# Attention's end reordered, attn_out into bank 2, and VectorE's background pieces ahead of the third mask

## The chip, the cores and the metric

The kernel runs on one core of one Trainium2 chip. The metric is the device time of one execution in microseconds (us); lower is better. TensorE (PE) multiplies and transposes into eight PSUM banks, VectorE (DVE), ScalarE (ACT) and GpSimd (POOL) do the elementwise work, and SyncE (SP) issues the DMAs. Each engine takes its instructions strictly in program order and waits on counting semaphores.

## The reference

One decoder layer on x of shape (4, 512, 512): causal attention with 32 query heads in 8 key groups, a cross product with a quantised context, and a mixture of experts. Cut to what matters:

```
x = x + attn(layernorm(x)):   q, k, v = x @ wq, x @ wk, x @ wv; rope on q and k
                              out = softmax(mask(q k^T / 8)) v, heads joined, @ wo
x = x + xattn(layernorm(x)):  8-bit rounding of x in blocks of 128 and of the context
                              in blocks of 128x128, then the product of the two
x = x + moe(layernorm(x)):    probs = softmax(xt @ Wg); eidx = argmax; place in its expert's
                              256 rows; silu(xd W1) * (xd W3) @ W2, plus the same of a
                              shared expert (sw1, sw3, sw2)
```

## The kernel before

**Attention** is a loop over `h` in `range(NH + 7)`, NH = 128, written out once for each engine; I call one value of `h` a step. A head is one batch and one four-head group's query head; four heads make a unit (`NU` = 32). Head `h` goes down a pipeline that is spread over several steps. On TensorE a step holds, in this order: `scores(h, 3)` and `scores(h, 2)` (banks 0 and 1), two thirds of the step's projection for a later unit, `weigh(h - 3)` (probabilities times values, bank 5), `turn_p(h - 2, 0)` (the probabilities of head h-2 turned, first of three parts, into bank 2), `scores(h, 1)`, `turn_p(h - 2, 1)` (bank 3), `scores(h, 0)`, `turn_p(h - 2, 2)` (bank 4), the rest of the projection, and `attn_out(h - 7)`, which multiplies a finished tile by wo. The steps whose unit index ends a cycle (k = 0, where k = (h + 8) mod 4) also turn the values (`turn_v`, L512). Steps with h of 120 and more have no projection. An fp32r product is made of three matmuls (`three`, L484 to L486).

**The banks of `attn_out`.** It writes bank 5, the bank of `weigh`, and bank 7 from n = NH - 11 = 117 on. So before it writes, `join` of head h-3 must have read bank 5 (`wait_bank5`), and before the next `weigh` writes, VectorE's `attn_out` (the add to X, L1269) must have read it.

**VectorE's step** is: `inverse_sums(h - 1)`, then the background pieces of some steps (`context_max`, `steps_of`, `large_steps_of`, `look`, the scales), then `masked(h, 3)`, `masked(h, 2)` (L1219, which ScalarE's `exp` waits for), per-unit work (`key_cos`, `value_lo`, `rotate`, `split_wo_lo`), `masked(h, 1)`, `join(h - 3)` (L1254, reads bank 5 and what ScalarE's `lower_out` left in Otmp), a side slot, `pt_lo(h - 2, 0)` (L1260, the last reader of bank 2), `masked(h, 0)`, `pt_lo` of parts 1 and 2, `rotate`, and the add of `attn_out(h - 7)`.

**The side slots** hold the later stages, batch by batch: `slots()` is a table of slot numbers for each stage. From step 117 on each step runs two slots (numbers 2(h - 117) - 44 and - 43), the first of them between `join` and `pt_lo(h - 2, 0)`. After the loop come slots -8, -7, -6, and then one slot with each eighth of a half batch `x` of the shared expert. `stats2` are row statistics for the second layernorm, `norm2` its root, `look` and `peaks` its block maxima, `scales`, `scaled` and `cross_round` the rounding (GpSimd does the last three operations, L1703 to L1707), `cross_turn` and `cross_product` the product with the context. Context jobs and the rounding for batch 0 run as a background during steps 59 to 124.

The weights of the shared expert are split into a high and a low part in pieces (`split_piece`), two in each step after h = 130 and the rest after the loop.

Of the kernel before, what the change touches and what calls it, by code (L numbers as in the profile page):

```python
# [10 lines left out]
NU = NG * NB  # L11
# [24 lines left out]
def slots():  # L36
# [17 lines left out]
    plan(-2, "logits", 0)  # L54
    plan(0, "choose", 0)
    plan(3, "place", 0)
    for b in range(1, NB):
        s = 16 * (b - 1)
        for i in range(TB):
            plan(s - 13 + i, "stats2", b, i)  # L60
            if b > 1:
                plan(s - 4 + i + i // 3, "context_turn", b, i)
# [16 lines left out]
        plan(s + (19 if b < NB - 1 else 15), "place", b)  # L79
    for i in range(2):  # L80
        plan(16 * NB - 13 + i, "load_x", i)
        plan(16 * NB - 9 + i, "expert_turn", 0, i)
# [20 lines left out]
def decoder(nc, x_in, ctx_in, wqkv_in, wo_in, wg_in, wf_in, ident_in, mask_in, rope_in, ksin_in, rank_in, tri_in, out):  # L103
# [3 lines left out]
    with ExitStack() as root:  # L107
# [170 lines left out]

        def set_of(x):
            return 0 if x < NX else x - NX + 1  # L280
# [38 lines left out]
        PT_BLOCKS = [[(0, qb) for qb in range(4)], [(1, 1), (1, 2), (1, 3), (3, 3)], [(2, 2), (2, 3)]]  # L319

# [61 lines left out]
        def wait_piece_free(need, m, p):  # L382
            if m == 0 and p < UP:
                need.wait_ge(p_pv, NH)
            elif m == 0:
                wait_attention(need)
# [34 lines left out]
        def wait_bank5(need, h, user):  # L421

            if user == "attn_out":
                need.wait_ge(a_tmp, h - 2)
                need.wait_ge(v_join, h - 2)
            elif h < 8 or h - 8 >= NH - 11:
                need.wait_ge(a_tmp, h - 3)
                need.wait_ge(v_join, h - 3)
            else:
                need.wait_ge(v_x, h - 7)  # L430
# [39 lines left out]
        def tensor_engine(e):  # L470
# [68 lines left out]
            def weigh(h):  # L539
# [7 lines left out]
                wait_bank5(need, h + 3, "weigh")  # L547
# [21 lines left out]
            def attn_out(n):  # L569
# [3 lines left out]
                ps = bank[7 if late else 5][:, :]  # L573
# [3 lines left out]
                if not late:  # L577
                    wait_bank5(need, n + 7, "attn_out")
                elif n == NH - 11:
                    wait_part(need, NU - 1, 2)  # L580
                else:
                    need.wait_ge(v_x, n)
# [101 lines left out]
            def ffn(x, k):  # L684
# [8 lines left out]
                if k < 6:  # L693
# [3 lines left out]
                    if x == 0 and k < 3:  # L697
                        wait_attention(need)
# [41 lines left out]
            for h in range(NH + 7):  # L740
# [32 lines left out]
                if 52 <= h < 60:  # L773
                    need.wait_ge(a_pt, 3 * (h - 2) + 1)
                    need.wait_ge(v_pt, 3 * (h - 2) + 1)
                    first_turn(h - 44, 2)
# [14 lines left out]
        def scalar_engine(e):  # L791
# [117 lines left out]
            def look_later(b, i):  # L909

                need.wait_ge(v_small, 3 + 2 * b)
                if i == 3:
                    need.wait_ge(p_kv, NU)
                    need.wait_ge(g_t2, TB * (b - 1))
# [70 lines left out]
            def split_piece(m, p):  # L985
                n = NP * m + p
                need.wait_ge(d_ring[n % NR], 16 * (n // NR + 1))
                wait_piece_free(need, m, p)
# [11 lines left out]
            def ffn(x, k, split):  # L1000
                m = set_of(x)
                if k < 6:
# [4 lines left out]
                    if x == 0 and k < 2:  # L1007
                        wait_attention(need)
# [37 lines left out]
            for h in range(NH + 7):  # L1046
# [53 lines left out]
                if 52 <= h < 60:  # L1100
                    first_turn(h - 44, 2)
                if h >= SIDE:
                    side_slot(2 * (h - SIDE) - 43)
                if h > NH + 2:
                    for _ in range(2):
                        split_piece(0, pieces.pop(0))
            for s in (-8, -7, -6):
                side_slot(s)
            while len(pieces) > NP - UP:
                split_piece(0, pieces.pop(0))  # L1110
            need.wait_ge(d_k, 48)
            need.wait_ge(g_const, 1)
            e.activation(Gh[:, :, 0:8], Graw[:, :, :], ACT.Copy).then_inc(a_const, 1)
            e.activation(trib[:, :], tri[:, :], ACT.Copy, accum_out=code[:, TB:TB + 1]).then_inc(a_const, 1)
# [14 lines left out]
        def vector_engine(e):  # L1129
# [133 lines left out]
            def attn_out(n):  # L1263
# [5 lines left out]
                e.tensor_tensor(X[:, t, :], X[:, t, :], bank[7 if n >= NH - 11 else 5][:, :], ALU.add).then_inc(v_x, 1)  # L1269
# [152 lines left out]
            def side_slot(s):  # L1422
                ends = []
                for x in side.get(s, ()):
# [7 lines left out]
                    elif stage in ("norm2", "rstd3"):  # L1432
                        rstd_of(slice(b * TB, (b + 1) * TB))
                        if stage == "norm2":
                            bias_of(b)
                    elif stage == "peaks":
# [112 lines left out]
            for h in range(NH + 7):  # L1549
# [4 lines left out]
                if h >= 0 and h % 8 == 0 and 0 < h // 8 + 1 <= NSAVE:  # L1554
                    split_wq_lo(h // 8 + 1)
                if h in takes:
# [11 lines left out]
                if 0 <= h < NH:  # L1568
                    masked(h, 3)
                    masked(h, 2)  # L1570
                if after_unit and k == 0:
# [602 lines left out]
```

## Time and profile before

| | us |
|---|---|
| three runs | 1531.92, 1531.93, 1536.74; median 1531.93 |
| the profiled execution | 1532.62, of which its instructions span 1530.8 |
| PE busy | 1437.9 (94%) |
| DVE, ACT, POOL busy | 1147.5 (75%), 984.9 (64%), 1027.0 (67%) |

Times in the rows are microseconds from the start of the profiled span. "Busy" of PE is modelled and its matmuls overlap, so the start-to-start distance of two matmuls says more than their duration. The arrow in square brackets names what ended an engine's idle time. One step of attention is the distance between two starts of the first `scores` matmul (L502, 128x512).

### The profile page before, as it was taken

What the parts mean: (1) busy time and instruction counts of PE and PEld (TensorE: products, weight loads), DVE (VectorE), ACT (ScalarE), POOL (GpSimd) and SP (SyncE); (2) the same over time, 40 slices, a digit from 0 to 9 for tenths busy, and PEclk for the clock granted to TensorE, in tenths of its full rate; (3) what the DMA queues carried; (4) which work ended last, traced back from release to release, by engine and by line L of the source; (5) the groups of instructions that cost most, each with busy time, mean ns of one, the idle gap of its engine ahead of it and who ended that gap; (6) DMA issues with size and microseconds to landing.
All of it is one profiled execution on the core that took longest, in us unless ns stands there. A gap on an engine that the chain in (4) does not pass through costs nothing.

```text
span 1530.8 us, 26938 instructions
## 1 busy us (share of the span) xinstructions
PE 1437.9 (94%) x8617; PEld 1259.0 (82%) x8617; DVE 1147.5 (75%) x2820; ACT 984.9 (64%) x2509; POOL 1027.0 (67%) x1043
## 2 busy tenths in 40 slices
PE   5899999999999999999999999897898999999997
PEld 3778888888878888778888888776787888999996
DVE  7678888887887887887888788787565754677773
ACT  4687786777776887878878787756141412555562
POOL 3787888888877788888898888644404131366663
PEclk9999999999999999999999999999999999999998
DMA  6445454334322424334234342504111011587772
GB/s 209 116 122 166 124 147 134 87 111 124 84 80 63 112 75 128 88 83 123 73 113 126 82 132 66 169 1 147 43 35 49 22 43 39 170 267 236 253 244 80
DMA packets 108620, 174.74 MB, mean 114 GB/s; under 512 B 20936, under 2 KB 42696, under 8 KB 108480
## 3 DMA queue, kind: packets, MB, share of 16 engines
q1 hardware_dynamic: 104448, 160.51, 36.0%
q0 software_dynamic: 3840, 12.25, 2.1%
q8 instruction: 70, 1.15, 0.3%
q14 instruction: 70, 0.57, 0.1%
q10 hardware_dynamic: 192, 0.26, 0.1%
HBM read 94.05 MB, written 33.18 MB: 83 GB/s over the span
## 4 chain that ended last, share of the span: by engine, by line
PE 66%; ACT 12%; DVE 11%; issue 5%; DMA 2%; POOL 2%; SPq 1%; DVEq 0%; POOLq 0%; ACTq 0%
PE bank L484 15%; PE bank L486 14%; PE bank L485 14%; PE bank L536 5%; ACT P L875 5%; PE bank L551 4%; PE bank L552 3%; PE bank L502 3%; PE bank L503 3%; DVE P L1219 2%; ACT PTh L887 2%; PE bank L476 2%; ACT Otmp L881 2%; DVE PTl L1260 1%; DVE Opair L1254 1%
## 5 line engine op out<-in xcount | busy, mean ns | idle before, releaser
L875 ACT ACTIVATE P<-P,mn 128x512 f32<-128x512 f32 (+3 forms) x512 | 284.5, 557 | 206.9 <-DVE mn L1219 203.1
L1660 POOL TENSOR_TENSOR P<-P,ri 128x128 f32<-128x128 f32 (+3 forms) x512 | 360.7, 737 | 30.7 <-DVE ri L1208 30.7
L1219 DVE CUSTOM_DVE_ANT_0 P<-bank,mask 128x512 f32<-128x512 f32 (+3 forms) x512 | 236.6, 480 | 84.3 <-PE bank L503 82.8
L1260 DVE TENSOR_TENSOR PTl<-bank,PTh 128x512 fp32r<-128x512 f32 (+1 forms) x384 | 229.8, 599 | 34.1 <-ACT PTh L887 31.1
L536 PE MATMUL bank<-ident,P 128*128 128x128 f32 x1280 | 202.6, 273 | 2.5 <-POOL P L1660 2.5
L887 ACT ACTIVATE PTh<-bank 128x512 fp32r<-128x512 f32 (+1 forms) x384 | 198.1, 517 | 3.9 <-PE bank L536 1.0
L502 PE MATMUL bank<-KT,QT 128*128 128x256 f32 (+2 forms) x512 | 188.1, 368 | 6.4 <-DVE mn L1219 6.4
L484 PE MATMUL bank<-XT,Wh 128*128 128x512 f32 x384 | 163.8, 427 | 8.1 <-DVE XT L1190 3.5
L503 PE MATMUL bank<-KT,QT 128*128 128x256 f32 (+2 forms) x512 | 166.0, 324 | 0.0
L551 PE MATMUL bank<-PTh,VS 128*128 128x256 f32 (+2 forms) x512 | 161.1, 326 | 5.2 <-DVE X L1269 2.4
L552 PE MATMUL bank<-PTl,VS 128*128 128x256 f32 (+2 forms) x512 | 154.5, 324 | 0.0
L486 PE MATMUL bank<-XT,Wl 128*128 128x512 f32 x384 | 152.9, 398 | 0.0
L485 PE MATMUL bank<-XT,Wh 128*128 128x512 f32 x384 | 152.6, 397 | 0.0
L536 PEld LDWEIGHTS bank<-ident,P 128*128 128x128 f32 x1280 | 150.1, 141 | 3.0 <-POOL P L1660 3.0
L1698 POOL TENSOR_TENSOR OTl<-Opair,OTh 128x512 fp32r<-128x512 f32 x64 | 83.6, 1306 | 94.7 <-ACT OTh L958 93.9
L484 PE MATMUL bank<-Oh,OTh 128*128 128x512 f32 x256 | 106.0, 414 | 20.9 <-DVE Opair L1254 15.5
L1254 DVE TENSOR_TENSOR Opair<-bank,Otmp 64x512 f32<-64x512 f32 x128 | 87.4, 683 | 39.8 <-ACT Otmp L881 38.5
L502 PEld LDWEIGHTS bank<-KT,QT 128*128 128x128 f32 x512 | 96.8, 189 | 21.2 <-DVE mn L1219 8.9
L1011 ACT ACTIVATE hm<-bank 128x256 f32<-128x256 f32 x96 | 36.4, 379 | 117.8 <-PE bank L486 117.0
L551 PEld LDWEIGHTS bank<-PTh,VS 128*128 128x128 f32 x512 | 96.2, 188 | 19.4 <-issue 6.7
L503 PEld LDWEIGHTS bank<-KT,QT 128*128 128x128 f32 x512 | 97.5, 190 | 10.5
L552 PEld LDWEIGHTS bank<-PTl,VS 128*128 128x128 f32 x512 | 96.1, 188 | 10.0
(225 smaller groups left out, 4090.2 us busy)
## 6 DMA issues: line engine op xcount, KB each, us to landing
RW<-in_wf SPq DMA_DIRECT2D x153, 256.0 KB, 3.4
QT<-qh SPq DMA_DIRECT2D x256, 64.0 KB, 2.0
QT<-ql SPq DMA_DIRECT2D x252, 64.0 KB, 2.0
Oraw<-in_wo SPq DMA_DIRECT2D x16, 512.0 KB, 4.8
KT<-KT SPq DMA_DIRECT2D x32, 256.0 KB, 3.0
Wraw<-in_wqkv SPq DMA_DIRECT2D x9, 768.0 KB, 4.7
xnx<-in_ctx SPq DMA_DIRECT2D x24, 256.0 KB, 3.5
saved<-Wh SPq DMA_DIRECT2D x7, 768.0 KB, 3.5
```

The costliest lines, as they stand in the source:

```text
L484: e.matmul(ps, lh, rh, start=start, stop=False)
L485: e.matmul(ps, lh, rl, start=False, stop=False)
L486: return e.matmul(ps, ll, rh, start=False, stop=stop)
L502: e.matmul(ps[:, 0:k], lhs, KT[:, u % 2, 0, 0:k], start=True, stop=False)
L503: e.matmul(ps[:, 0:k], lhs, KT[:, u % 2, 1, 0:k], start=False, stop=True).then_inc(p_s, 1)
L536: last = e.transpose(ps[:, tokens(m)], src, ident[:, :])
L551: e.matmul(ps[:, q:512], lhs, pt_of(PTh, kb), start=kb == 0, stop=False)
L552: last = e.matmul(ps[:, q:512], lhs, pt_of(PTl, kb), start=False, stop=kb == 3)
L875: e.activation(pq, pq, ACT.Exp, bias=mn[:, z, qb:qb + 1], scale=-1.0, accum_out=rs[:, z, qb:qb + 1]).then_inc(a_exp, 1)
L1219: e.tensor_tensor_reduce(P[:, z, off[qb]:off[qb] + k], bank[n % 2][:, 0:k], mask[:, 512 - k:512], -0.125, BIG, ALU.add, ALU.min, mn[:, z, ...
L1260: e.tensor_tensor(pt_part(PTl, part), bank[2 + part][:, 0:128 * n].rearrange("p (m n) -> p m n", n=128), pt_part(PTh, part).bitcast(F32), ...
L1660: e.tensor_tensor(pq, pq, ri[:, z, qb:qb + 1].to_broadcast([128, n]), ALU.mult).then_inc(g_norm, 1)
```

## The change

- **Output bank.** `attn_out` writes bank 2 (`out_bank`) for n < 117, then bank 7, and for n = 125 and 127 bank 2 again. Before it writes bank 2 it waits for both readers of `turn_p(n + 5, 0)`: in step h that is `pt_hi` and `pt_lo` of head h-2, part 0. The next step's `turn_p(.., 0)` waits for VectorE's add, and `weigh` for `join` of the head before it alone.
- **VectorE's step.** The masks 3 and 2 come first. The add (now of tile h - 8, for n < 117), the per-unit work, and then the background pieces stand between mask 2 and mask 1.
- **First turns** of steps 52 to 59 go to bank 5 in place of bank 2.
- **Batch 1's side stages** are planned apart: `stats2` in slots -44, -42, -40, -38 (steps 117 to 120) in place of -13 to -10; the root is started on VectorE in slot -36 and finished by GpSimd's `newton` in slots -34 to -28; `look` at -14, `peaks` at -12, `scales` at -8 in place of -8, -7 and -4; the four roundings one or two slots sooner. `logits`, `choose` and `place` of batch 0 move from -2, 0, 3 to -6, -4, -2.
- **Pieces and constants.** Eleven pieces are split in steps 128 to 133. The router's weights and constants are loaded in step 125 and prepared in steps 128 to 130, and a first Silu is run in step 129.

The core of the diff (the slot table, `pieces_at`, `bias_of` on GpSimd and the waits on counts that go with them are left out):

```
+        def out_bank(n):
+            return bank[2 if n < NH - 11 or n >= NH - 4 and n % 2 else 7]
...
@@ turn_p
-                if part == 0 and 51 <= h < 59:
-                    wait_xt(need, h - 42)
+                if part == 0 and 0 <= h - 6 < NH - 11:
+                    need.wait_ge(v_x, h - 5)
@@ weigh
-                wait_bank5(need, h + 3, "weigh")
+                wait_bank5(need, h + 3)
@@ attn_out on TensorE
-                ps = bank[7 if late else 5][:, :]
+                ps = out_bank(n)[:, :]
...
                 if not late:
-                    wait_bank5(need, n + 7, "attn_out")
+                    need.wait_ge(a_pt, 3 * (n + 5) + 1)
+                    need.wait_ge(v_pt, 3 * (n + 5) + 1)
                 elif n == NH - 11:
                     wait_part(need, NU - 1, 2)
-                else:
+                elif n <= NH - 4:
                     need.wait_ge(v_x, n)
+                else:
+                    need.wait_ge(a_pt, 3 * NH)
+                    need.wait_ge(v_pt, 3 * NH)
+                    need.wait_ge(v_x, n - 1)
@@ ScalarE's loop
+                if h == NH + 1:
+                    need.wait_ge(d_k, 48)
+                    need.wait_ge(g_const, 1)
+                    e.activation(Gh[:, :, 0:8], Graw[:, :, :], ACT.Copy).then_inc(a_const, 1)
+                    e.activation(trib[:, :], tri[:, :], ACT.Copy, accum_out=code[:, TB:TB + 1]).then_inc(a_const, 1)
+                    e.activation(wam[:, 0, 0:1], wam[:, 0, 0:1], ACT.Silu)
@@ VectorE's loop
+                if 0 <= h < NH:
+                    masked(h, 3)
+                    masked(h, 2)
+                if 0 <= h - 8 < NH - 11:
+                    attn_out(h - 8)
+                if after_unit and k == 0:
+                    key_cos(unit - 1)
...
                 if h in takes:
                     context_max(takes[h])
...
-                if 0 <= h < NH:
-                    masked(h, 3)
-                    masked(h, 2)
...
-                if 0 <= h - 7 < NH:
+                if NH - 11 <= h - 7 < NH:
                     attn_out(h - 7)
```

How the order stands now. First VectorE in step 106, before and then after the change (`ISA` is the mask, L1219 before and L1259 after; PTl<-bank2 is `pt_lo` part 0; X<-X,bank5 or bank2 is the add):

```order
L1208 RECIPROCAL ri<-rs 128x4 [waits a_exp]
L1219 ISA P,mn<-bank0,mask 128x512 [waits p_pt,p_s]
L1219 ISA mn 128x1
L1219 ISA P,mn<-bank1,mask 128x384 [waits p_s]
L1219 ISA mn 128x1
L1232 TENSOR_TENSOR qcs<-bank6,rope 128x512
L1219 ISA P,mn<-bank0,mask 128x256 [waits p_s]
L1219 ISA mn 128x1
L1254 TENSOR_TENSOR Opair<-bank5,Otmp 64x512 [waits a_tmp]
L1260 TENSOR_TENSOR PTl<-bank2,PTh 128x512 [waits p_pv,a_pt]
```

```order
L1248 RECIPROCAL ri<-rs 128x4 [waits a_exp]
L1259 ISA P,mn<-bank0,mask 128x512 [waits p_pt,p_s]
L1259 ISA mn 128x1
L1259 ISA P,mn<-bank1,mask 128x384 [waits p_s]
L1259 ISA mn 128x1
L1309 TENSOR_TENSOR X<-X,bank2 128x512 [waits v_x,p_ao]
L1272 TENSOR_TENSOR qcs<-bank6,rope 128x512
L1259 ISA P,mn<-bank0,mask 128x256 [waits p_s]
L1259 ISA mn 128x1
L1294 TENSOR_TENSOR Opair<-bank5,Otmp 64x512 [waits a_tmp]
L1300 TENSOR_TENSOR PTl<-bank2,PTh 128x512 [waits p_pv,a_pt]
```

The add, which stood ahead of the reciprocal, stands behind mask 2; `join` and `pt_lo` keep their place behind mask 1.

TensorE at the end of a step, before and after (bank 4 and 6 are the last turned part and the projection, Oh with OTh is `attn_out`):

```order
L536 MATMUL bank4<-ident,P 128x128 x2
L484 MATMUL bank6<-XT0,Wh 128x512
L485 MATMUL bank6<-XT0,Wh 128x512
L486 MATMUL bank6<-XT0,Wl 128x512
L484 MATMUL bank5<-Oh,OTh 128x512 [waits v_join,a_tmp]
L485 MATMUL bank5<-Ol,OTh 128x512
```

```order
L563 MATMUL bank4<-ident,P 128x128 x2
L511 MATMUL bank6<-XT0,Wh 128x512
L512 MATMUL bank6<-XT0,Wh 128x512
L513 MATMUL bank6<-XT0,Wl 128x512
L511 MATMUL bank2<-Oh,OTh 128x512 [waits v_pt,a_pt]
L512 MATMUL bank2<-Ol,OTh 128x512
```

The output keeps its place in TensorE's order; its wait moved from `join` to the `pt_lo` that stands behind `join` on VectorE.

VectorE in step 118 after the change (before it, the two middle rows stood near the loop's end):

```order
L1294 TENSOR_TENSOR Opair<-bank5,Otmp 64x512 [waits a_tmp]
L1202 BN_STATS st<-X 128x6
L1204 BN_AGGR mv<-st 128x2 [waits v_own]
L1300 TENSOR_TENSOR PTl<-bank2,PTh 128x512 [waits p_pv,a_pt]
L1259 ISA P,mn<-bank1,mask 128x128 [waits p_s]
```

Batch 1's statistics now stand between `join` and the `pt_lo` that `attn_out` waits for.

## Rows read from the trace of the kernel before

**Rows 1.** Windows: stretch, its length, busy PE, PEld, DVE, ACT, POOL, PEclk, DMA, GB/s.
```profile
98.90:951.60 852.70, 832.46 (x4739) 715.35 (x4738) 696.98 (x1843) 662.79 (x1751) 720.41 (x761) 1.00 0.38 106
...
1012.50:1049.00 36.50, 27.86 (x151) 22.78 (x150) 31.17 (x70) 18.96 (x40) 16.00 (x16) 0.95 0.20 61
1049.00:1098.70 49.70, 40.06 (x233) 35.26 (x234) 32.93 (x78) 21.09 (x50) 23.20 (x27) 0.93 0.26 80
```

**Rows 2.** Waits in 98.9 to 951.6, TensorE's, then VectorE's: total, times, longest.
```profile
PE bank L484 <- DVE Opair L1254: 13.7, 26, 1.2
PE bank L484 <- DVE XT L1190: 2.0, 1, 2.0
DVE P L1219 <- PE bank L503: 67.7, 80, 2.0
```

**Rows 3.** Timeline, TensorE: first turn in step 57; first matmuls of steps 104 to 108.
```profile
474.24 0.60 PE L476 MATMUL bank<-ident,xnx 128*128 128x128 f32 x4
...
831.68 0.39 PE L502 MATMUL bank<-KT,QT 128*128 128x512 f32 x1
...
839.40 0.39 PE L502 MATMUL bank<-KT,QT 128*128 128x512 f32 x1
...
846.51 0.39 PE L502 MATMUL bank<-KT,QT 128*128 128x512 f32 x1
...
853.64 0.39 PE L502 MATMUL bank<-KT,QT 128*128 128x512 f32 x1
...
861.19 0.39 PE L502 MATMUL bank<-KT,QT 128*128 128x512 f32 x1
```

**Rows 4.** Timeline, step 105: mask 1, join, pt_lo part 0, and TensorE's attn_out.
```profile
843.75 0.42 DVE L1219 CUSTOM_DVE_ANT_0 P<-bank,mask 128x256 f32<-128x256 f32 x1 [1.19 <-PE bank L503]
...
844.10 0.68 DVE L1254 TENSOR_TENSOR Opair<-bank,Otmp 64x512 f32<-64x512 f32 x1
...
844.70 0.67 DVE L1260 TENSOR_TENSOR PTl<-bank,PTh 128x512 fp32r<-128x512 f32 x1
...
845.13 0.39 PE L484 MATMUL bank<-Oh,OTh 128*128 128x512 f32 x1
```

**Rows 5.** Timeline, step 106: join, pt_lo part 0, and attn_out.
```profile
851.33 0.69 DVE L1254 TENSOR_TENSOR Opair<-bank,Otmp 64x512 f32<-64x512 f32 x1
852.04 0.69 DVE L1260 TENSOR_TENSOR PTl<-bank,PTh 128x512 fp32r<-128x512 f32 x1
...
852.25 0.39 PE L484 MATMUL bank<-Oh,OTh 128*128 128x512 f32 x1
```

**Rows 6.** Timeline, step 107: a join that comes late and the attn_out that waits.
```profile
858.90 0.68 DVE L1254 TENSOR_TENSOR Opair<-bank,Otmp 64x512 f32<-64x512 f32 x1 [0.47 <-ACT Otmp L881]
...
859.73 0.47 PE L484 MATMUL bank<-Oh,OTh 128*128 128x512 f32 x1 [0.18 <-DVE Opair L1254]
```

**Rows 7.** Timeline, step 85: its first matmul, a late lower_out, and attn_out behind it.
```profile
687.62 0.39 PE L502 MATMUL bank<-KT,QT 128*128 128x512 f32 x1
...
693.01 0.60 ACT L881 ACTIVATE Otmp<-bank 64x512 f32<-64x512 f32 x1
...
694.46 0.47 PE L484 MATMUL bank<-Oh,OTh 128*128 128x512 f32 x1 [0.93 <-DVE Opair L1254]
```

**Rows 8.** Timeline, VectorE in step 127: statistics between join and pt_lo.
```profile
1016.79 0.68 DVE L1162 BATCH_NORM_STATS2 st<-X 128x6 f32<-128x512 f32 x1
...
1017.60 0.67 DVE L1260 TENSOR_TENSOR PTl<-bank,PTh 128x512 fp32r<-128x512 f32 x1
```

**Rows 9.** TensorE's waits in the whole span (the last two attn_outs); timeline, first expert matmul.
```profile
PE bank L484 <- DVE X L1269: 3.4, 2, 2.3
...
1049.01 0.36 PE L484 MATMUL bank<-XT,Uh 128*128 128x256 f32 x1 [1.31 <-issue]
```

**Rows 10.** Timeline: ScalarE's table load and TensorE's longest wait behind it.
```profile
1058.42 1.28 ACT L1011 ACT_TABLE_LOAD   x1
...
1073.61 1.08 PE L476 MATMUL bank<-ident,work 128*128 128x128 f32 x4 [5.48 <-POOL work L1707]
```

More of the change, by code:

```diff
@@ L53, in slots @@
     plan(-23, "rstd3", 0)
[L54 to L57, printed above, removed]
+    plan(-6, "logits", 0)
+    plan(-4, "choose", 0)
+    plan(-2, "place", 0)
+    plan(3, "scatter", 0)
+    for i in range(TB):
+        plan(-44 + 2 * i, "stats2", 1, i)
+        plan(-14 + i, "look", 1, i)
+        plan(-12 + i, "peaks", 1, i)
+        at = (-4, -3, -1, 1)[i]
+        plan(at - 1, "scaled", 1, i)
+        plan(at, "cross_round", 1, i)
+        plan((-1, 0, 1, 3)[i], "cross_turn", 1, i)
+        plan((0, 1, 2, 4)[i], "cross_product", 1, i)
+        plan((1, 2, 3, 5)[i], "stats3", 1, i)
+        plan(7 + i // 2, "norm3", 1, i)
+        plan(9 + i // 2, "route_turn", 1, i)
+    plan(-36, "first_root", 1)
+    for i in range(3):
+        plan(-34 + 2 * i, "root", 1, i)
+    plan(-28, "bias", 1)
+    plan(-8, "scales", 1)
+    plan(6, "rstd3", 1)
+    plan(12, "logits", 1)
+    plan(14, "choose", 1)
+    plan(19, "place", 1)
+    plan(19, "scatter", 1)
+    for b in range(2, NB):
         s = 16 * (b - 1)
@@ L1100, in scalar_engine @@
                 if 52 <= h < 60:
-                    first_turn(h - 44, 2)
+                    first_turn(h - 44, 5)
                 if h >= SIDE:
                     side_slot(2 * (h - SIDE) - 43)
-                if h > NH + 2:
-                    for _ in range(2):
-                        split_piece(0, pieces.pop(0))
+                for _ in range(pieces_at.get(h, 0)):
+                    split_piece(0, pieces.pop(0))
+                if h == NH + 1:
[4 more added lines that the diff above has]
+                    e.activation(wam[:, 0, 0:1], wam[:, 0, 0:1], ACT.Silu)
             for s in (-8, -7, -6):
                 side_slot(s)
[L1109 to L1114, printed above, removed]
             for x in range(NX):
@@ L1268, in attn_out @@
                     need.wait_ge(v_x, n - 7)
-                e.tensor_tensor(X[:, t, :], X[:, t, :], bank[7 if n >= NH - 11 else 5][:, :], ALU.add).then_inc(v_x, 1)
+                e.tensor_tensor(X[:, t, :], X[:, t, :], out_bank(n)[:, :], ALU.add).then_inc(v_x, 1)
             def scales(amax, r, d, least):
@@ L1555, in vector_engine @@
                     split_wq_lo(h // 8 + 1)
+                if 0 <= h < NH:
[5 more added lines that the diff above has]
+                    key_cos(unit - 1)
+                if after_unit and k == 1:
+                    value_lo(unit - 1)
+                if unit < NU and k == 2:
+                    rotate(unit, 0, 1)
+                if h >= 15 and h % 8 == 7 and h // 8 < NEP:
+                    split_wo_lo(h // 8)
                 if h in takes:
@@ L1610, in vector_engine @@
                 if 52 <= h < 60:
-                    first_turn(h - 44, 2)
+                    first_turn(h - 44, 5)
                 if h >= SIDE:
                     side_slot(2 * (h - SIDE) - 43)
-                if h > NH + 2:
-                    for _ in range(2):
-                        split_piece(0, pieces.pop(0))
+                for _ in range(pieces_at.get(h, 0)):
+                    split_piece(0, pieces.pop(0))
             for s in (-8, -7, -6):
                 side_slot(s)
-            while len(pieces) > NP - UP:
-                split_piece(0, pieces.pop(0))
             for x in range(NX):
```

124 lines of the change are left out of this document (69 added, 55 removed).

## The prediction

> **What bounds the kernel now.** I read the windows first: in the stretch of steps 8 to 119 (98.9 to 951.6, 112 steps) TensorE is busy 832.46 of 852.70 us at full granted clock, so that stretch is worth what TensorE's own order costs, plus its waits [rows 1]. The mean step is 852.7 / 112 = 7.61 us. A step without a wait shows TensorE's own length: step 105 took 846.51 - 839.40 = 7.11, step 106 took 7.13, and step 104, which also turns the values, 7.72 [rows 3]. Four such steps (a unit) make 7.72 + 7.11 + 7.13 + 7.12 = 29.08, and 28 units 814.2. So some 38 us of the stretch are waits and eight extra transposes. The waits view names the largest: `attn_out` behind VectorE's `join`, 13.7 us in 26 waits [rows 2]. From 1012.5 to 1098.7 the picture changes: TensorE is idle 8.6 of 36.5 and 9.6 of 49.7 us, and its granted clock falls to 0.95 and 0.93 of full (between its two levels, 2.4 and 1.2 GHz) [rows 1]. So there are two places with something to win, and the first has some 110 steps in which a small loss counts each time.
>
> **Part 1: the output in bank 2, steps 8 to 119.** Where TensorE does not wait, it reaches `attn_out` 845.13 - 839.40 = 5.73 us after the step's start in step 105, and 852.25 - 846.51 = 5.74 in step 106 [rows 3 to 5]. What it must wait for is now `pt_lo` part 0, which stands behind `join` on VectorE. In step 105 this starts at 844.70, in step 106 at 852.04 [rows 4, 5]. From the start of such a VectorE operation to the start of a waiting `attn_out` it takes 859.73 - 858.90 = 0.83 us, as the late `join` of step 107 shows [rows 6]. So `attn_out` could start at 845.53 and 852.87: 0.40 and 0.62 later than now. Could VectorE be sooner there? The reordering gives it time before mask 1, but mask 1 already waits for TensorE's own `scores(h, 1)`: 1.19 us in step 105 [rows 4], and 67.7 us in 80 waits of this kind in the stretch [rows 2]. The chain from `scores(h, 1)` over mask 1 (starts 4.35 into the step), `join` (4.70) and `pt_lo` (5.30) is closed and holds nothing that the change shortens. And a TensorE that has waited restarts a little slower: from `attn_out` to the next step 861.19 - 859.73 = 1.46 against 853.64 - 852.25 = 1.39 [rows 3, 5, 6]. The new step lengths: 6.13 + 1.46 = 7.59 where h is odd, 6.36 + 1.46 = 7.82 where k = 2. Where k = 0 the values' transposes bring TensorE there only at 7.72 - 1.39 = 6.33 against some 6.36, so 7.72 to 7.84; I take 7.80. A unit: 7.80 + 7.59 + 7.82 + 7.59 = 30.80, and 28 of them 862.4.
>
> To this come the eight first turns of steps 52 to 59, at most 0.60 each [rows 3]; they overlap what follows, and I take 8 x 0.47 = 3.8 (they only change their bank), and what stays of today's waits. The masks and with them ScalarE's exponentials come 0.6 to 1.5 us sooner, so most joins are no longer late, and background pieces fit into VectorE's wait at mask 1 (0.6 to 0.9 us of work against 1.2 to 2 us). What stays: the projection that waits for a first turn, 2.0 today [rows 2], and a second one like it, together 2.2 of some 3.5, since the add no longer stands ahead of the turn; five steps in which ScalarE itself is late. Step 85 is the pattern: ScalarE comes to `lower_out` only 693.01 - 687.62 = 5.39 into the step, since its scaling of the block before runs until then, and `attn_out` waits until 694.46 - 687.62 = 6.84 [rows 7]. With the masks sooner I put it at 5.05; then `join` follows 0.63 later, `pt_lo` 0.61 after that and `attn_out` 0.83 after that, at 7.12: later than now, though ScalarE is sooner. The step grows from 6.84 + 1.46 = 8.30 to 8.58, 1.0 over the new 7.59. Five such steps at 0.8 make 4.0; VectorE's chains of small scale operations in two or three steps 0.8. Sum 7.0. So steps 8 to 119 take 862.4 + 3.8 + 7.0 = 873.2 against 852.7: **+20.5**. Step 7, the first with an output, +0.4. Bounds: without all that stays, and with k = 0 steps at 7.72, 28 x 30.72 + 3.8 = 864.0, +11; with 0.04 more for the new second wait of each `turn_p` part 0, +25. That second wait itself is met in time: the add ends about 2.6 into the step, and `turn_p` starts at 3.5.
>
> **Part 2: steps 117 to 123.** Batch 1's statistics stand between `join` and `pt_lo`: 1017.60 - 1016.79 = 0.81 us each [rows 8], in steps 117 to 120. With `attn_out` now behind that `pt_lo`, all of it is on the path in 117 to 119: 2.4. Steps 120 to 122 have no projection and run round the same chain: the three VectorE operations ahead of `turn_p` end that wait some 2.8 into the step, mask 1 follows at 3.7, `join` at 4.2, statistics or a context turn, `pt_lo` at 5.7, the output 0.83 later, the next step 1.46 after it, at 8.0. These are estimates from the distances of part 1; against today's lengths I count +0.9, +0.4 and +0.2. Step 123 waits for a transfer anyway; I put its output's wait at +0.7. Together **+4.6** (3 to 6). Steps 124 to 127 write bank 7 and keep their length.
>
> **Part 3: attention's end and the first half batch.** The last two outputs wait 3.4 for the add, the first expert matmul 1.31 more [rows 9]. Alternate banks and earlier pieces remove these 4.7. Something is given back: in step 129 ScalarE now does a table load of 1.28 [rows 10], two small copies and two pieces ahead of the last `lower_out`, and the outputs hang on the pair that follows it. I count 1.3, so -3.4. From 1049.0 to 1098.7 TensorE idles 9.6 and loses up to 3.5 to the clock (0.07 x 49.7) [rows 1]; the largest wait, 5.48, is for GpSimd's rounding of the first block of batch 1 [rows 10]. In the new table `scales` come four slots sooner, the rounding two, the turn one, so the rounding has a slot of some 3 us more, and ScalarE's first Silu no longer waits for the router's weights. I leave 3.0 of these 13.1: -10.1. Sum **-13.5** (from -20, all that both stretches have but the wait for the pair, to -9). Everything after 1098.7 is the same work in the same order: 0.
>
> On the table load the row shows 1.28 us and the next activation right behind it, at 1.29. The Trainium skill ("ScalarE: Activation LUTs", "What ACT_TABLE_LOAD costs") adds a drain of about 1380 ns to each switch, 2.66 us in all. By the page the outputs would come 1.4 later and the sum would be 1.4 higher; by the row they do not. I go by the row.
>
> **The sum.** 20.5 + 0.4 + 4.6 - 13.5 = +12.0. The profiled execution took 1532.62, so 1544.6; the median of the runs is 0.7 below it, so **1544**. About 0.3%, 4.6 us, is what a measurement of this kernel can tell from no change (1527.3 to 1536.5).
>
> **The rivals.**
> - *The tail pays for it.* If nothing of today's late joins stays (+11), the statistics cost 3 and the tail gives 18 to 20, the sum is -4 to -6, 1527. For it: 18.2 us are idle there. Against it: VectorE is busy 31 of 36.5 us in 1012.5 to 1049 [rows 1], which its new order doesn't lessen, and step 85's kind stays. Between this and my forecast lies no measurable change, 1532. Chance 0.12 for the latter, 0.03 for the former.
> - *Faster: VectorE's relief wins.* This holds if `pt_lo` part 0 is ready by 5.73 into the step, that is if mask 1 can start 0.4 us (0.62 in even steps) sooner than 4.35. Then steps 8 to 119 take 814.2 + 3.8 + 7.0 = 825, -28, and with parts 2 and 3 the time is 1532 - 28 + 2 - 13 = 1493. Half of this effect would give 1520. The 80 waits of mask 1 for TensorE speak against it. Chance 0.05.
> - *Worse: the clock.* TensorE now idles 0.4 to 0.6 us in every step. If the granted clock fell in the loop as it does in the tail, to 0.98 on the mean, 852.7 x 0.02 = 17 us would come on top, 1561. The trace has steps with waits of 1 to 2 us in this stretch at a granted 1.00 [rows 1, 2], which speaks against. The Trainium skill ("TensorE: Matmul & The Clock Gate", "A second HAM failure mode: psum-queue depth-cycling") describes short idles at bank changes that make the clock oscillate, and would have this rival; the trace so far disagrees. Chance 0.04.
> - *The move does nothing in the loop.* If `attn_out` hardly waits for VectorE at all and today's joins are still late, the loop stays at 852.7 and the time is 1532 + 3 - 13 = 1522. It needs a wait that TensorE's order does not have. Chance 0.02.
>
> **How the numbers follow.** The forecast, 1544, has what remains, 0.74. Its own range goes from +11 + 0.4 + 3 - 14 to +25 + 0.4 + 6 - 10, which is 1532 to 1553; with the no-change rival taken in at its upper part I give 1533 to 1552 for 8 in 10. Slower by over 0.3%: 0.74 + 0.04 less 0.02 for the part of its own range below 1536.5, 0.76. Within 0.3%: 0.12 + 0.02 = 0.14. Faster: 0.03 + 0.05 + 0.02 = 0.10.
>
> **What would show it.** In the profile after, TensorE's waits must name PTl (`pt_lo`) ahead of L511's `attn_out` in nearly every step, with hardly a wait for Opair; steps of 7.59, 7.82, 7.59 and about 7.8; mask 3 at about 0.9 into most steps, mask 1 still at 4.35 with a longer wait for TensorE; steps 117 to 119 of 8.4 and more; the last outputs without a wait for X; the wait before batch 1's first turn under 2 us. If steps of 7.12 remain, part 1 is wrong; if the stretch after attention doesn't shrink by 8 to 16 us, part 3 is.

## The result, and the profile after

The changed kernel takes 1584.5 us (median of 4 runs, 1583.5 to 1585.24) against 1532.66 for the kernel before (4 runs): 1.034 times as long, with a 95% interval of 1.032 to 1.035. The forecast was 1544. Its sign was right, its size was not: 52 us were lost, not 12. The profiled execution has a span of 1583.2 us, at a mean granted clock of 0.984.

The windows, with the columns of [rows 1]. The first is steps 8 to 119, from first matmul to first matmul; the second is steps 113 and 114; the last two follow the last step of the loop.

```profile
94.90:1001.10 906.20, 849.29 (x4739) 715.57 (x4738) 731.22 (x1850) 665.03 (x1752) 722.50 (x763) 0.99 0.36 99
934.50:958.70 24.20, 17.49 (x84) 14.57 (x83) 19.73 (x35) 10.12 (x28) 13.50 (x14) 0.79 0.34 96
1068.50:1100.00 31.50, 25.26 (x138) 21.80 (x137) 26.67 (x57) 19.76 (x43) 15.95 (x23) 0.89 0.18 57
1100.00:1152.00 52.00, 43.67 (x266) 38.28 (x265) 38.51 (x75) 20.28 (x49) 26.36 (x22) 0.97 0.30 102
```

The same number of matmuls (x4739) that took 852.7 us in [rows 1] now takes 906.2. The waits in steps 8 to 119, first TensorE's, then VectorE's (total, times, longest), answer to [rows 2]:

```profile
PE bank L511 <- DVE PTl L1300: 52.5, 84, 6.2
PE bank L563 <- DVE X L1309: 2.3, 6, 0.4
PE bank L511 <- DVE XT L1230: 1.4, 1, 1.4
...
DVE P L1259 <- PE bank L530: 115.2, 126, 2.0
```

The wait for Opair is gone, and one for PTl (`pt_lo`) has taken its place, in most steps. Now one step as [rows 3, 4] show it. The first matmuls of steps 105 to 108:

```profile
870.29 0.40 PE L529 MATMUL bank<-KT,QT 128*128 128x512 f32 x1
...
877.88 0.39 PE L529 MATMUL bank<-KT,QT 128*128 128x512 f32 x1
...
885.71 0.39 PE L529 MATMUL bank<-KT,QT 128*128 128x512 f32 x1
...
893.30 0.39 PE L529 MATMUL bank<-KT,QT 128*128 128x512 f32 x1
```

Step 105 takes 7.59, step 106 7.83, step 107 7.59. Inside step 105, VectorE and then TensorE:

```profile
872.98 1.09 DVE L1366 TENSOR_SCALAR Zb<-Zb 128x512 f32<-128x512 f32 x1
874.65 0.43 DVE L1259 CUSTOM_DVE_ANT_0 P<-bank,mask 128x256 f32<-128x256 f32 x1 [0.58 <-PE bank L530]
875.00 0.08 DVE L1259 DVE_READ_ACCUMULATOR2_ANT mn<- 128x1 f32 x1
875.00 0.68 DVE L1294 TENSOR_TENSOR Opair<-bank,Otmp 64x512 f32<-64x512 f32 x1
875.60 0.67 DVE L1300 TENSOR_TENSOR PTl<-bank,PTh 128x512 fp32r<-128x512 f32 x1
...
876.42 0.47 PE L511 MATMUL bank<-Oh,OTh 128*128 128x512 f32 x1 [0.23 <-DVE PTl L1300]
```

Mask 1 still waits for TensorE (at 4.36 into the step), `join` at 4.71, `pt_lo` at 5.31, `attn_out` at 6.13 where it could have started at 5.73. This is the closed chain of the forecast, to 0.01 us.

Where the 52 us lie, by the profiled executions, each stretch from first matmul to first matmul:

| stretch | before | after | difference | forecast |
|---|---|---|---|---|
| start to step 8 | 98.92 | 94.93 | -4.0 | +0.4 |
| steps 8 to 119 | 852.65 | 906.14 | +53.5 | +22.9 |
| steps 120 to 123 | 34.08 | 39.37 | +5.3 | +2.2 |
| steps 124 to 126 | 26.88 | 27.20 | +0.3 | 0 |
| step 127 to the end | 518.31 | 515.52 | -2.8 | -13.5 |

In step 113 there is something that the kernel before does not have at all. VectorE, GpSimd and TensorE there:

```profile
936.51 7.79 DVE L1361 TENSOR_SCALAR Zb<-xnx 128x512 uint32<-128x512 uint32 x1
944.22 0.41 DVE L1259 CUSTOM_DVE_ANT_0 P<-bank,mask 128x256 f32<-128x256 f32 x1
```
```profile
936.45 1.29 POOL L1779 TENSOR_TENSOR xnx<-xnx,Zb 128x512 f32<-128x512 f32 x1
937.69 2.39 POOL L1713 TENSOR_TENSOR ql<-qcs,qh 128x1024 fp32r<-128x1024 f32 x1
940.03 2.75 POOL L1701 TENSOR_TENSOR P<-P,ri 128x128 f32<-128x128 f32 x4
942.74 1.27 POOL L1784 TENSOR_TENSOR xnx<-xnx,Zb 128x512 f32<-128x512 f32 x1
948.14 2.76 POOL L1701 TENSOR_TENSOR P<-P,ri 128x128 f32<-128x128 f32 x4 [4.13 <-DVE ri L1248]
```
```profile
945.98 0.77 PE L511 MATMUL bank<-Oh,OTh 128*128 128x512 f32 x1 [6.23 <-DVE PTl L1300]
946.54 0.63 PE L512 MATMUL bank<-Ol,OTh 128*128 128x512 f32 x1
946.97 0.63 PE L513 MATMUL bank<-Oh,OTl 128*128 128x512 f32 x1
```

A VectorE piece that elsewhere takes 0.41 us stands for 7.79 us. It ends 0.3 us after the last of GpSimd's operations that follow each other without a gap (942.74 + 1.27 = 944.01). Behind it everything is late: TensorE waits 6.23 us, and when it starts again its matmuls follow each other every 0.43 us in place of 0.23: the granted clock has gone to the lower of its two levels (1.2 in place of 2.4 GHz) for a while, 0.79 on the mean of these two steps.

### The profile page after: what moved, and what is told of

Its sections match the earlier page's. It is cut to its first block, busy times and chain, and to the rows that moved or that the text cites. A ratio compares the mean times of both kernels' runs of the same rounds, so it can differ in the third digit from the quotient of the medians.

```text
span 1583.2 us, 27143 instructions
## 1 busy us (share of the span) xinstructions
PE 1457.0 (92%) x8617; PEld 1261.6 (80%) x8617; DVE 1181.7 (75%) x2810; ACT 987.1 (62%) x2510; POOL 1031.4 (65%) x1057
## 4 chain that ended last, share of the span: by engine, by line
PE 68%; DVE 16%; issue 7%; ACT 6%; DMA 2%; POOL 1%; SPq 1%; DVEq 0%; POOLq 0%; ACTq 0%
PE bank L511 16%; PE bank L512 15%; PE bank L513 15%; DVE PTl L1300 4%; PE bank L563 4%; PE bank L578 4%; PE bank L579 4%; PE bank L529 4%; PE bank L530 4%; DVE Opair L1294 3%; DVE P L1259 2%; PE bank L503 2%; ACT P L912 1%; DMA Oraw<-in_wo 1%; DVE X L1309 1%
## 5 line engine op out<-in xcount | busy, mean ns | idle before, releaser
L1701 POOL TENSOR_TENSOR P<-P,ri 128x128 f32<-128x128 f32 (+3 forms) x512 | 364.8, 745 | 33.8 <-DVE ri L1248 31.1
L1259 DVE CUSTOM_DVE_ANT_0 P<-bank,mask 128x512 f32<-128x512 f32 (+3 forms) x512 | 238.3, 484 | 136.4 <-PE bank L530 130.3
L511 PE MATMUL bank<-Oh,OTh 128*128 128x512 f32 x256 | 112.7, 440 | 62.5 <-DVE PTl L1300 60.5
L511 PEld LDWEIGHTS bank<-Oh,OTh 128*128 128x128 f32 x256 | 48.7, 190 | 111.8 <-ACT PTh L924 57.5
L918 ACT ACTIVATE Otmp<-bank 64x512 f32<-64x512 f32 x128 | 76.4, 596 | 70.1 <-PE bank L579 69.0
L529 PEld LDWEIGHTS bank<-KT,QT 128*128 128x128 f32 x512 | 97.5, 190 | 15.4 <-DVE mn L1259 2.7
```

Of the source, the lines that this page charges most:

```text
L511: e.matmul(ps, lh, rh, start=start, stop=False)
L529: e.matmul(ps[:, 0:k], lhs, KT[:, u % 2, 0, 0:k], start=True, stop=False)
L1259: e.tensor_tensor_reduce(P[:, z, off[qb]:off[qb] + k], bank[n % 2][:, 0:k], mask[:, 512 - k:512], -0.125, BIG, ALU.add, ALU.min, mn[:, z, ...
L1701: e.tensor_tensor(pq, pq, ri[:, z, qb:qb + 1].to_broadcast([128, n]), ALU.mult).then_inc(g_norm, 1)
```

## The experiments

All times are medians; each run is compared with runs of the kernel before on the same chip (1533.3, 1533.3 and 1533.7 us in the three groups; 1532.7 beside the changed kernel, so the kernel before itself moves by up to 1 us between groups). Two theories stood at first: A, the bank is the loss; B, the moved pieces are. Three kernels undo one part or both, and a fourth turns one order.

**e1: bank 5 again.** The pieces stay where the change put them, the tail too.

```
             def out_bank(n):
-                return bank[2 if n < NH - 11 or n >= NH - 4 and n % 2 else 7]
+                return bank[5 if n < NH - 11 else 2 if n >= NH - 4 and n % 2 else 7]
...
-                need.wait_ge(a_pt, 3 * (n + 5) + 1)
-                need.wait_ge(v_pt, 3 * (n + 5) + 1)
+                wait_bank5(need, n + 7, "attn_out")
```

> The changed kernel with one part undone: attn_out writes bank 5 again with the old waits (behind the previous join, not behind pt_lo), VectorE's add stands at the step's end again, the eight first turns of steps 52 to 59 are back in bank 2. VectorE's pieces stay between mask 2 and mask 1, the new tail stays. Theory A (the bank is the loss: in every step attn_out waits for join and then pt_lo): steps of 7.12 (k = 1, 2, 3) and 7.73 (k = 0) come back, 45 us over steps 8 to 112 are gained, the time is 1535 to 1542. Theory B (the moved pieces are most of the loss, because they now meet GpSimd's work and delay mask 1): the time stays above 1565. If both weigh alike, about 1555.

Measured: 1531.9 us, ratio to before 0.999 (0.998 to 1.0). Theory A: 52.6 us of the loss hang on the bank, its waits, the add's place and the first turns' bank, which go together here. It went 3 us below the 1535 expected.

**e2: the pieces back at the step's head**, bank 2 kept.

```
                     split_wq_lo(h // 8 + 1)
+                if h in takes:
+                    context_max(takes[h])
...
+                if h - 4 in begins:
+                    large_steps_of(begins[h - 4])
                 if 0 <= h < NH:
                     masked(h, 3)
```

> The changed kernel with the other part undone: VectorE's pieces are back at the step's head, ahead of mask 3; bank 2, the moved add, the new tail stay. Theory A: the steps without background work stay at 7.59 and 7.83, and the late joins of the kernel before come on top where pieces are; the 7.79 us operation of step 113 is gone. Time 1572 to 1590. Theory B: most of the 52 us goes, time under 1555.

Measured: 1583.5, ratio 1.032 (1.030 to 1.034). Theory B falls: with the pieces back nothing is gained. But theory A's "the 7.79 us operation is gone" was only half right: another one has come up at the step's head, in step 114 (minimum, median and maximum of this line in ns):

```profile
L1366 DVE TENSOR_SCALAR Zb<-Zb x20: 394/738/5071, 535.8 to 1000.2; 128x512 f32<-128x512 f32 x20
```

**e3: both undone, the tail alone.**

> The changed kernel with both parts of the loop undone: the attention loop is that of the kernel before, and only the new side-slot table, the earlier pieces and loads and the alternating last banks stay. Both theories: the traces show 2.8 us gained behind the last mask, nothing else, so 1529 to 1531 against 1532.7. If the tail's changes lost something inside the loop (batch 1's statistics in steps 117 to 120 and three root rounds on GpSimd), 1533 to 1536. My prediction on record had 13.5 us of gain here, which would be 1519.

Measured: 1532.2, ratio 0.999 (0.998 to 1.0). The time lies between the two that I had expected. The tail is worth 1 us, within what can't be told from nothing. In its profile the stretch from step 127 on is 3.3 us shorter than before (515.04 against 518.31) and steps 117 to 123, which now carry batch 1's statistics, are 3.6 longer (59.4 against 55.9). With e1 the two halves of the change are laid out: bank 2 costs 52.6 us with the pieces moved (1584.5 - 1531.9) and 51.3 without (1583.5 - 1532.2); moving the pieces is worth 0.3 in bank 5 and costs 1.0 in bank 2, neither clear of the spread of the runs.

**e4: `pt_lo` ahead of `join`.** If the chain mask 1, `join`, `pt_lo` sets the step, one turned order should free it.

```
+                swap = 7 <= h < NH - 4
+                if swap:
+                    pt_lo(h - 2, 0)
                 if 0 <= h - 3 < NH:
                     join(h - 3)
...
-                if 0 <= h - 2 < NH:
+                if 0 <= h - 2 < NH and not swap:
                     pt_lo(h - 2, 0)
```
(and the same for ScalarE's `pt_hi` and `lower_out`.)

> The changed kernel with one order turned in steps 7 to 123: VectorE does pt_lo part 0 ahead of join, and ScalarE its pt_hi part 0 ahead of lower_out; bank 2 and everything else stay. Theory A: attn_out then hangs on one VectorE operation after mask 1 and not on two; pt_lo can start about 4.75 into the step, attn_out about 5.6, at or just before TensorE gets there (5.74). Steps of 7.1 to 7.3, time 1540 to 1552. Theory B: mask 1 is the late one, so the gain is under 12 us, time over 1572. A third way: ScalarE's swapped order makes pt_hi late or join late for the next weigh, and the gain is half, 1560.

Measured: 1564.3, ratio 1.019 (1.016 to 1.022). The step is what theory A says: the undisturbed ones are 7.12 to 7.14 and 7.73 again, `attn_out` starts at 5.74 to 5.76. Steps 8 to 50 gain 15.4 us. Yet the total gains 20 and not 32 to 44, and the rows of the exponent pieces tell why:

```profile
L1369 DVE TENSOR_SCALAR Zb<-Zb x20: 417/855/6548, 520.5 to 987.3; 128x512 f32<-128x512 f32 x20
L1364 DVE TENSOR_SCALAR Zb<-xnx x10: 417/936/7983, 513.0 to 922.2; 128x512 uint32<-128x512 uint32 x10
```

Seven of the 40 exponent pieces stand for 3.4 to 8.0 us, 36 us more than undisturbed ones. They became the question. In e1 there are such too, in step 69 for one; VectorE's row, then GpSimd's:

```profile
552.40 4.29 DVE L1368 TENSOR_SCALAR Zb<-Zb 128x512 f32<-128x512 f32 x1
```
```profile
551.48 1.30 POOL L1739 TENSOR_TENSOR OTl<-Opair,OTh 128x512 fp32r<-128x512 f32 x1
552.74 1.28 POOL L1784 TENSOR_TENSOR xnx<-xnx,Zb 128x512 f32<-128x512 f32 x1
553.98 2.37 POOL L1713 TENSOR_TENSOR ql<-qcs,qh 128x1024 fp32r<-128x1024 f32 x1
556.32 2.98 POOL L1701 TENSOR_TENSOR P<-P,ri 128x128 f32<-128x128 f32 x4
```

Theory C: GpSimd holds off VectorE's operations that read and write only the chip's SBUF, for as long as GpSimd has one ready operation behind the other. Rival D: they are slow for a reason of their own. The test takes no work away; it makes GpSimd pause.

```
+                if h - 3 in begins:
+                    need.wait_ge(v_bm, begins[h - 3] + 1)
+                if h - 4 in begins:
+                    need.wait_ge(v_bq, begins[h - 4] + 1)
                 if after_unit and k == 1:
                     query_lo(unit - 1)
                 if 0 <= h - 1 < NH:
                     normalised(h - 1)
```

**e5: the pause in the changed kernel.**

> The changed kernel with one wait added on GpSimd, in steps in which VectorE has one of the exponent pieces (L1361, L1366): GpSimd starts its next operation only when that piece is done. No work changes. Theory C (VectorE's SBUF-only pieces start only when GpSimd pauses, and GpSimd's row of ready operations holds them off: 7.79 us for a 0.41 us operation in step 113): no such piece takes over 2 us any more, step 113 falls from 14.9 to about 7.6, step 114 from 9.3 to 7.8, and the time is 1573 to 1577. Rival D (the operation was slow for a reason of its own, such as its data or its code being fetched): it stays near 7.8 us and the time stays at 1583 to 1586, or more for the wait.

Measured: 1574.3, ratio 1.028 (1.026 to 1.031). Step 113 is 7.59 long again, steps 113 and 114 fell from 24.2 to 15.4 us together, and no exponent piece takes over 1.51. Theory C, 10.2 us. Steps 83 and 84 fell too, from 19.0 to 15.5: in step 83 of the changed kernel small scale operations and an exponent piece stood beside GpSimd's four parts of `normalised` (L1701), two of the scale operations took 0.61 and 0.87 us and the piece 1.34, where they take 0.17, 0.17 and 0.42 with the pause. So steps 8 to 119 are 12.9 us shorter. Part of it is lost again in step 121 (13.47 against 10.11), which has no pause for this operation of batch 1's root:

```profile
1000.16 3.76 DVE L1183 TENSOR_SCALAR mv<-mv 128x4 f32<-128x4 f32 x1
```

In the changed kernel it took 0.15 us. Here GpSimd's operations follow each other until 1003.88, and it ends at 1003.92.

**e6: the pause with `pt_lo` first.**

> The same wait on GpSimd in the kernel with pt_lo part 0 ahead of join. There six pieces took 3.4 to 8.0 us. Theory C: 25 us of 1564 go, most of them on the path: 1540 to 1546, steps of 7.12, 7.73. Rival D: 1562 to 1567.

Measured: 1530.6, ratio 0.998 (0.997 to 1.0); 34 us less than e4, nearly all of the 36 us by which the seven pieces there were too long. I had expected 25, having left room for what hides behind mask 1's wait; the time is 9 us below the range. TensorE's clock behind each long wait is part of the difference: the windows of e4 show 0.94 for 530 to 560 us and 0.91 for 560 to 600, those of e6 1.00 for 525 to 595. Against the kernel before, this one is no loss and no gain. That does not clear bank 2: the kernel with the same pieces, pause and tail and with bank 5 (e7) is 11.8 us faster. In steps 8 to 50 bank 2 costs 6.1 us (320.0 against 313.9), nearly all in the steps in which mask 3 comes late and the add holds up `turn_p` (step 16 takes 8.88 against 7.73), in steps 51 to 60 another 2.7.

**e7: the pause with bank 5.**

> The same wait on GpSimd in the kernel with attn_out back in bank 5 and VectorE's pieces ahead of mask 1. There steps 69, 93, 105 and 117 took 9.13 in place of 7.12, and step 81 13.1. Theory C: 12 to 14 us go, 1517 to 1521, which would beat both kernels. Rival D: 1530 to 1534.

Measured: 1518.8 (1518.5 to 1519.4), ratio 0.991 (0.989 to 0.992). This beats both kernels. Step 69 here, VectorE, then GpSimd:

```profile
554.19 2.12 DVE L1368 TENSOR_SCALAR Zb<-Zb 128x512 f32<-128x512 f32 x1
```
```profile
554.75 1.28 POOL L1784 TENSOR_TENSOR xnx<-xnx,Zb 128x512 f32<-128x512 f32 x1
556.39 2.40 POOL L1713 TENSOR_TENSOR ql<-qcs,qh 128x1024 fp32r<-128x1024 f32 x1 [0.37 <-DVE Zb L1368]
```

GpSimd's operation ends at 556.03 and the next one now waits; VectorE's piece, ready since 554.19, ends at 556.31, within the 0.37 us of the pause. The step is 7.13 long (9.14 in e1).

**e8: `pt_lo` first, pieces at the head, no pause.**

> The changed kernel with pt_lo part 0 ahead of join, and VectorE's pieces back at the step's head. Theory A: the steps without pieces stay at 7.12 and 7.73 as in the run with pt_lo first. Theory C: at the head the pieces meet GpSimd while it waits for VectorE's reciprocals, so few of them are held off, and the time is 1540 to 1550. If the position does not matter for the port, 1560 to 1566 as with the pieces behind mask 2.

Measured: 1568.6, ratio 1.022 (1.019 to 1.025). My expectation for theory C missed: at the head pieces are held off too, though fewer: two take 5.51 and 6.47 us (seven took over 3.3 in e4), and one takes 5.07 in e2. What this gives back is lost ahead of step 8 (3.2 us more than in e4) and in steps 8 to 50 (3.8 more). That none was held off at the head in the kernel before, where the longest took 1.58, is no property of the place. Why GpSimd leaves a gap there in the one kernel and not in the others I did not settle.

**e9: the fastest kernel, batch 0's router back in its old slots.**

```
-    plan(-6, "logits", 0)
-    plan(-4, "choose", 0)
-    plan(-2, "place", 0)
+    plan(-2, "logits", 0)
+    plan(0, "choose", 0)
+    plan(3, "place", 0)
```

> On the fastest kernel so far (bank 5, pieces ahead of mask 1, GpSimd's wait; 1518.8): batch 0's logits, choose and place back in their old side slots (-2, 0, 3); the rest of the new side-slot table stays. Theory E (the tail gave 3 of the 13.5 us that I forecast because batch 0's router chain of small VectorE operations now stands ahead of batch 1's rounding): the first expert matmul comes 1.5 us sooner, batch 1's first turn 3 us or more, and the time is 1513 to 1516. Rival F (what limits batch 1 is its own chain over VectorE and GpSimd, or TensorE's clock after the waits): 1518 to 1520, or more if the router now comes late for the second expert block.

Measured: 1516.8 (1515.2 to 1519.2), ratio 0.989 (0.987 to 0.991). Counted from the last step's mask 3, the first expert matmul comes 1.4 us sooner than in e7 and the second expert block's products 0.8; the total is 2.0 lower than e7's, in overlapping ranges and between what E and F expected. It points to E in sign, to F in size, and I leave it undecided.

**e10: the kernel before with pieces moved and pause, nothing else.**

> The kernel before with two edits only: VectorE's pieces between mask 2 and mask 1, and GpSimd's wait for them. Bank 5, old tail. If pieces and wait are what gained, and the tail's share is 1 to 3 us as in the runs above: 1519 to 1523.

Measured: 1518.9 (1517.1 to 1521.8), ratio 0.991 (0.989 to 0.993), the same as e7. So the new tail is worth nothing here either, and two small edits to the kernel before give 14 to 15 us. By the profiled executions 4.8 of them lie ahead of step 8, where the moved `context_max` no longer holds up mask 3, and 11.1 in steps 8 to 119.

**e11: the pause alone.**

> The kernel before with GpSimd's wait alone; the pieces stay at the step's head. There the longest of them took 1.58 us, so theory C leaves at most 5 us to gain: 1528 to 1534. If the wait gained 13 us by itself, whatever the pieces' place, theory C would have the wrong cause.

Measured: 1534.4, ratio 0.9995 (0.998 to 1.001). Neither edit is worth anything alone: the pause without the move gives 0, the move without the pause 0.3 (e1 against e3, both with the new tail). Together they give 14.

**e12: the add back at the end of VectorE's step**, bank 2 and pause kept (against e5).

```
-                if 0 <= h - 8 < NH - 11:
-                    attn_out(h - 8)
...
-                if NH - 11 <= h - 7 < NH:
+                if 0 <= h - 7 < NH:
                     attn_out(h - 7)
```

> The changed kernel with GpSimd's wait (1574.3), and the add of attn_out back at the end of VectorE's step, bank 2 kept. If turn_p part 0's wait for the add costs what step 16 and its like show (0.6 us every eighth step, 7 us in steps 52 to 60), 1565 to 1570. If VectorE, which must now wait for the late attn_out at the step's end, is late for mask 3 in turn: mask 3 at 0.9 to 1.3 into each step, which still hides behind mask 1's wait, 1572 to 1578; over 1580 if it does not hide.

Measured: 1570.7, ratio 1.024 (1.022 to 1.026). 3.6 us less than e5: `turn_p`'s wait for the add is real and small. Steps 8 to 50 fall by 2.7 us; steps 51 to 60 stay at 84.9, so there the add was not what cost.

## Why the prediction was right, and where it failed

Measured and forecast differ by 40 us. Of these, 28.8 are waits of steps 8 to 119 that the prediction took for gone or didn't see, 10.7 are the tail, 3.4 steps 120 to 126, 1.7 the clean step; the start gave 4.4 back.

**Right: the chain and the clean step.** Forecast 7.59, 7.82, 7.59, about 7.80; measured 7.59, 7.83, 7.59, 7.83 to 7.85. 28 units of 30.86 are 864.1, against 862.4 forecast. e4 shows the cause by itself: with `pt_lo` ahead of `join` the steps are 7.12 again. Right, too: mask 1 still at 4.36, mask 3 early (at 0.65 into most steps, forecast about 0.9), no wait for Opair, steps 117 and 118 at 8.4 and 8.6.

**Wrong: "most joins are no longer late, and background pieces fit into VectorE's wait at mask 1".** This is the step that failed. Above the clean steps, the stretch of steps 8 to 119 had 38.4 us of waits before (852.65 - 814.2); I left 13.2 of them (3.8 for the first turns, 7.0 for what stays, 2.4 for the statistics) and 42.0 came (906.14 - 864.1). By kind:

| steps | forecast | measured over the clean length |
|---|---|---|
| 113, 114: piece held off by GpSimd, and the clock after it | 0 | 8.8 |
| 83, 84: a row of scale operations and a piece, drawn out beside GpSimd | 0 | 3.6 |
| 71, 87, 95, 111: two VectorE pieces ahead of mask 1 | 0 | 4.3 |
| 51 to 60: first turns | 3.8 | 7.8 |
| 67, 73, 79, 85, 91, 97, 103, 109: ScalarE late | 4.0 | 9.6 |
| 8, 16, 24, 32, 40, 48: late mask 3, then the add ahead of `turn_p` | 0 | 3.3 |
| 117 to 119: statistics ahead of `pt_lo` | 2.4 | 4.1 |
| the rest | 3.0 | 0.5 |

How much the earlier masks can really give is shown by e7, where the bank's cost and the held-off pieces are both away: the same stretch takes 843.4, so 29.2 of 38.4 us stay. The relief is 9.2, where I had counted 27.6 before the statistics. What stays is mostly the first turns (steps 51 to 60 take 83.0 us there, 10.0 over their clean length) and ScalarE's own lateness, which don't hang on where VectorE's pieces stand. Some 3.7 us are steps 71, 87, 95 and 111, which the move itself made longer (8.05 there, about 7.55 before). I had seen ScalarE's pattern in [rows 7], but for five steps; there are eight, and in two of them, 79 and 103, it works in another way: VectorE's `split_wo_lo` (L1244), ahead of mask 1, waits 2.6 and 1.9 us for ScalarE.

The third row of the table is step 87, VectorE after its mask 2:

```profile
728.88 1.73 DVE L1244 TENSOR_TENSOR Ol<-Oraw,Oh 128x512 fp32r<-128x512 f32 x1
730.53 1.50 DVE L1366 TENSOR_SCALAR Zb<-Zb 128x512 f32<-128x512 f32 x1
731.95 0.41 DVE L1259 CUSTOM_DVE_ANT_0 P<-bank,mask 128x256 f32<-128x256 f32 x1
```

I had priced a piece at 0.6 to 0.9 us against 1.2 to 2 us of room. Here two stand together, each stretched by GpSimd, and mask 1 starts 5.4 into the step, not 4.4. In the kernel before one of them stood at the head, where 1 us hardly mattered. The sixth row is step 16, VectorE and TensorE:

```profile
157.78 1.68 DVE L1238 TENSOR_TENSOR Wl<-Wraw,Wh 128x512 fp32r<-128x512 f32 x1
159.38 0.68 DVE L1259 CUSTOM_DVE_ANT_0 P<-bank,mask 128x512 f32<-128x512 f32 x1
...
160.47 0.68 DVE L1309 TENSOR_TENSOR X<-X,bank 128x512 f32<-128x512 f32 x1
```
```profile
161.29 0.63 PE L563 MATMUL bank<-ident,P 128*128 128x128 f32 x4 [0.42 <-DVE X L1309]
```

"That second wait is met in time: the add ends about 2.6 into the step" holds for clean steps only. Where a weight split (L1238) stands at the head, mask 3 starts at 2.15, the add ends at 3.92, and `turn_p` comes 0.6 late (161.29 in a step that began at 157.23). All of it reaches the step's end, since `join` and `pt_lo` follow from there. e12 puts this error at 2.7 us in steps 8 to 50 and at 3.6 in the whole time.

**Wrong: the tail, -13.5 against -2.8.** The waits that the forecast named did shrink. What came in their place, in the changed kernel after the last mask (total, times, longest):

```profile
PE bank L503 <- POOL work L1748: 4.3, 2, 2.2
...
PE bank L511 <- ACT YT L1005: 3.0, 1, 3.0
```

The wait of 5.48 for batch 1's rounding [rows 10] has become 4.3 in two pieces, and one of 3.0 for ScalarE's copy of a turned block (YT) comes behind them. The root of batch 1's statistics, the peaks and the scales stand sooner, but the wait for the rounding is only 1.2 us shorter. The first expert matmul now has batch 0's logits ahead of it and comes 1.8 us later after the last mask's start than before (37.4 against 35.6). The second batch of expert work is then 4.4 us ahead, of which 1.6 is lost again some 200 us after the last mask, where the windows show a granted clock of 0.97. And TensorE's clock is worse from the start, 0.89 in the first 31.5 us against 0.95 in [rows 1]. I counted removed waits as gained time without asking which chain is next. Whether that is batch 1's own chain or batch 0's logits ahead of it, e9 left undecided. e3 and e10 agree that the tail's edits are worth about nothing.

**Not foreseen: the start, -4.0.** A VectorE piece (`context_max`) at the head of an early step had waited 3.3 us for a transfer with mask 3 behind it. In its new place that wait stands behind masks 3 and 2 and is 1.2. With the pieces back at the head (e2) step 8 starts at 99.4 again, against 94.9.

**The table load.** In the tail ScalarE's rows read:

```profile
1088.31 1.28 ACT L1152 ACT_TABLE_LOAD   x1
1089.60 0.20 ACT L1152 ACTIVATE wam<-wam 128x1 f32<-128x1 f32 x1
```

The next activation starts 1.29 us after the load, as in the kernel before. The drain of some 1380 ns that the Trainium skill ("ScalarE: Activation LUTs", "What ACT_TABLE_LOAD costs") adds to a switch is not seen here either.

**The rivals.** "Worse: the clock" named the right symptom and the wrong condition. The delays of 0.4 to 0.6 us in every step left the clock alone: it is 1.00 on the mean of every window from 94.9 to 691. It fell behind longer waits: 6.23 us in step 113, 2.30 in step 83 (0.50 from 700 to 702), and in steps 119 to 121, with 1.8 to 2.5 in each; it did not fall behind the 2.75 of step 79. The oscillation at short idles that the Trainium skill ("TensorE: Matmul & The Clock Gate", "A second HAM failure mode: psum-queue depth-cycling") describes is thus not borne out by this loop. The other rivals had the wrong sign; none of them, and no term of the sum, had a VectorE operation that GpSimd makes longer.

## What to carry to other kernels

A wait that TensorE meets in every step costs its length times the steps, and this part could be forecast here to 0.01 us from one closed chain; but a credit for "the others will then no longer be late" must be worked out step by step, from what each late step really hangs on. Before moving a VectorE operation, look at what GpSimd runs at the new place, without a gap, and for how long. If a moved operation must stand there, let GpSimd wait for it: that one wait turned a change worth nothing (e1) into one worth 14 us (e7, e10). Then look at every other VectorE operation again, the small ones too: e5 lost 3.4 us in step 121 to one of 128x4.

## What the runs showed of the hardware

A VectorE operation with all its operands in SBUF (a `tensor_scalar` of 128x512 from SBUF to SBUF, 0.39 to 0.41 us when undisturbed) can take 4.29, 6.55, 7.79 or 7.98 us beside a row of GpSimd operations without gaps. In step 113 it ended 0.3 us after the last of them, and GpSimd's four rows there kept their usual 1.3, 2.4, 2.8 and 1.3 us. A small operation can lose as much: one of 128x4 took 3.76 us in place of 0.15 (step 121 of e5). It need not lose until then: in step 69 of e1 it got in between two of them, 0.3 us after `ql` ended, and GpSimd's next group took 2.98 in place of 2.75 us. Operations with PSUM among their inputs kept their durations beside GpSimd: in step 69 of e1 mask 1 took 0.41 us, `join` 0.68 and `pt_lo` 0.67 while GpSimd's group ran from 556.32 to 559.30. In the profile it looks like a long operation and not like a wait: no releaser is named, and the engine counts as busy. The Trainium skill ("SBUF — State Buffer", "Who interferes with whom") calls the SBUF port pair that VectorE and GpSimd share an exclusive lock that the first to start keeps for its whole instruction. The trace agrees that one of them blocks fully. It goes beyond the page in that GpSimd's next operation came first again and again while VectorE waited, through four rows of them in step 113. Whether another form of the same operation would have escaped was not tried.

The second is what such a wait does to TensorE: after 6.23 us of idle time its matmuls came every 0.43 us in place of 0.23 for some time, so the 7.4 us that the piece took too long cost 8.8 in all.
